# A transformer block with quantised feed-forward and routed experts: gathered token tiles transposed by DMA instead of TensorE

## The reference

```python
def reference(x, w1, w2, router_w, gate_proj, up_proj, down_proj):
    x = x + quantised_ffn(layernorm(x), w1, w2)     # per batch: int8 products of 512x512x512 and 512x256x512
    h = layernorm(x)
    p = softmax(h @ router_w)                       # 8 experts
    weights, chosen = top_k(p, 2)                   # 2 per token, weights normalised to 1
    for e in chosen experts of a token:
        x += weight[e] * ((silu(h @ gate_proj[e]) * (h @ up_proj[e])) @ down_proj[e])
    return x
```

## Time and profile before

| | us |
|---|---|
| median of 3 runs | 382.35 (381.81 to 384.08) |
| profiled execution | 381.06 |
| its span, first to last instruction | 379.3 |
| PE busy in the span | 321.9 |
| first late gather starts | 217.69 |
| last 12 matmuls of "up" (tile 38) start | 362.56 |

### The profile page before, as it was taken

How to read it: one execution, slowest core, us unless ns; L and a number is a source line. 1 busy time by engine, 2 the same in 40 slices (tenths; PEclk the granted TensorE clock), 3 DMA queues, 4 the chain that set the end, 5 groups by cost and what they waited for, 6 DMA issues and landing times.

```text
span 379.3 us, 6450 instructions
## 1 busy us (share of the span) xinstructions
PE 321.9 (85%) x1955; PEld 189.8 (50%) x1955; DVE 225.1 (59%) x515; ACT 202.9 (54%) x382; POOL 244.5 (64%) x271
## 2 busy tenths in 40 slices
PE   4698757877798885679899899999999999999980
PEld 1455435545665652375574455555555555555530
DVE  3588887879899988878678732333333333333320
ACT  1557568888897796139635234444444444444430
POOL 6486697879999971685461472656667746675441
PEclk9999999999999999999999999999999999999997
DMA  7765446745765508147127554557687657786544
GB/s 247 245 264 196 136 163 199 265 147 165 277 258 188 189 35 242 64 167 232 75 31 275 86 144 80 101 99 116 129 137 115 125 95 123 132 137 107 92 55 55
DMA packets 27551, 56.79 MB, mean 150 GB/s; under 512 B 2624, under 2 KB 13888, under 8 KB 25600
## 3 DMA queue, kind: packets, MB, share of 16 engines
q0 software_dynamic: 8736, 20.45, 29.9%
q1 hardware_dynamic: 17968, 35.39, 27.0%
q10 hardware_dynamic: 816, 0.54, 0.5%
HBM read 37.50 MB, written 18.87 MB: 149 GB/s over the span
## 4 chain that ended last, share of the span: by engine, by line
PE 33%; POOL 22%; issue 17%; DVE 14%; ACT 5%; DMA 4%; POOLq 2%; SPq 0%; DVEq 0%; ACTq 0%
PE bank_h L1328 13%; PE bank_q L1349 6%; POOL x L648 4%; POOL w_in L666 3%; POOL out L687 3%; DVE amax L726 3%; PE bank_t L1313 3%; PE bank_q L1194 2%; POOL w_in L619 2%; POOL gu_lo L584 2%; DVE rmax L756 2%; POOLq L682 2%; PE bank_h L1222 2%; ACT xn L1014 2%; DMA stage<-tokens,gather_at 2%
## 5 line engine op out<-in xcount | busy, mean ns | idle before, releaser
L1328 PE MATMUL bank_h<-gu_hi,xT 128*128 x312 | 103.9, 379 | 0.0
L1328 PE MATMUL bank_h<-gu_lo,xT 128*128 x156 | 59.1, 379 | 0.0
L970 DVE SCALAR_TENSOR_TENSOR xT<-bank_t,xT 128x512 f16<-128x512 f32 x39 | 26.8, 689 | 53.9 <-ACT xT L1104 53.8
L1349 PE MATMUL bank_q<-dn_hi,aT 128*128 x156 | 52.6, 379 | 1.7 <-DVE aT L988 1.4
L1328 PEld LDWEIGHTS bank_h<-gu_hi,xT 128*128 128x128 f16 x312 | 30.5, 98 | 29.3 <-issue 0.2
L666 POOL DMA_INDIRECT w_in<-tokens,gather_at x30 | 29.8, 993 | 17.8 <-issue 7.6
L584 POOL TENSOR_TENSOR gu_lo<-stage,gu_hi 128x1024 bf16<-128x1024 f32 x16 | 34.0, 2135 | 7.5 <-ACT gu_hi L1061 7.3
L978 DVE SCALAR_TENSOR_TENSOR gated<-bank_h,gated 128x256 f32<-128x256 f32 x39 | 16.5, 422 | 32.0 <-ACT gated L1111 32.0
L1111 ACT ACTIVATE gated<-bank_h 128x256 f32<-128x256 f32 x39 | 14.9, 383 | 38.0 <-PE bank_h L1328 38.0
L726 DVE TENSOR_REDUCE amax<-bank_t 128x1 f32<-128x512 f32 x48 | 30.8, 684 | 6.6 <-PE bank_t L1194 4.7
L687 POOL DMA_INDIRECT out<-h,scatter_at x17 | 26.9, 1580 | 11.8 <-DMA out<-h,scatter_at 4.5
(11 more groups left out here) (197 smaller groups left out, 704.5 us busy)
## 6 DMA issues: line engine op xcount, KB each, us to landing
stage<-in_L_ffn_gate_proj SPq DMA_DIRECT2D x8, 512.0 KB, 4.2
stage<-in_L_ffn_up_proj SPq DMA_DIRECT2D x8, 512.0 KB, 4.1
stage<-in_L_ffn_down_proj SPq DMA_DIRECT2D x8, 512.0 KB, 4.9
x<-in_x SPq DMA_DIRECT2D x4, 1024.0 KB, 6.3
out<-x SPq DMA_DIRECT2D x4, 1024.0 KB, 4.6
tokens<-xn SPq DMA_DIRECT2D x4, 1024.0 KB, 4.5
x_in<-in_x SPq DMA_DIRECT2D x3, 1024.0 KB, 7.5
w_in<-in_fside_BxS2xS SPq DMA_DIRECT2D x3, 1024.0 KB, 5.6
```

Of the source, the lines that this page charges most:

```text
L970: dve.scalar_tensor_tensor(out=xT[i % 2][:, 1].rearrange("p c t -> p (c t)"), in0=bank, scalar=X_SCALE, in1=xT[i % 2][:, 0].rearrange("p c ...
L1328: ins = pe.matmul(bank, xT[i % 2][:, part, c], rhs[:, cols], start=(c == 0 and m == 0), stop=(c == C - 1 and m == 2))
L1349: ins = pe.matmul(bank, aT[i % 2][:, part, c], rhs[:, cols], start=(c == 0 and n == 0), stop=(c == FC - 1 and n == 2))
```

## The change

`tokens_dram` has rows of 1024 float16: 512 of the high half, 512 of the low half; a row still has 2 KB. The scale 256 moves into the layer norm (`deviation` for part 2). After `normalise 2` of a batch, ACT makes the high halves of the whole batch (`token_high`, one instruction, 128x2048), and DVE (batches 0, 2, 3) or POOL (batch 1) makes the low halves in place (`token_low`, one instruction, 128x2048). SP stores the halves with two DMAs; all that waited for the store of a batch waits for both. ACT's `x_high`, DVE's `x_low` and PE's transposes of tokens are gone, 39 of each; PE's list keeps the step "expert", which only reads the expert's number.

In their place SP has the steps "turn": one DMA transpose each of a gathered tile, 128x1024 float16 to `xT` as eight blocks of 128x128. The ring `xT` has four buffers; two of them lie in the old `xqT`. Turn i waits for gather i and, from i = 4 on, for "up" of tile i-4. Gather i+4 of the late tiles waits for turn i, and an early gather i+3 for turn i. The landings are no longer counted at the end of SP's list but as steps "landed" between the turns.

```diff
-            def x_low(i):
-                ...
-                dve.scalar_tensor_tensor(out=xT[i % 2][:, 1].rearrange("p c t -> p (c t)"), in0=bank, scalar=X_SCALE,
-                                         in1=xT[i % 2][:, 0].rearrange("p c t -> p (c t)"), op0=ALU.mult,
-                                         op1=ALU.subtract).then_inc(ring_t.taken, 1)
+            def token_low(b):
+                dve.wait_ge(sem("token_high"), b + 1)
+                dve.tensor_tensor(token_low_of, xn2[:], token_high_of(b), ALU.subtract).then_inc(sem(f"token_low{b}"), 1)
...
+            def token_high(b):
+                if b == 1:
+                    ring_q.done(act, "x transposed", C - 1, B - 1)
+                elif b > 1:
+                    act.wait_ge(sem(f"tokens_stored{b - 1}"), 32)
+                act.wait_ge(sem("xn2_ready"), upto(b, J))
+                act.activation(token_high_of(b), xn2[:], ACT.Copy).then_inc(sem("token_high"), 1)
...
+            def turn(i):
+                sp.wait_ge(gathered(i), 16 * times_gathered(i))
+                if i == 0:
+                    sp.wait_ge(sem("xn_ready"), upto(B - 1, J))
+                if i == len(xT_in):
+                    ring_h.done(sp, "product 1", J - 1, B - 1)
+                if i >= TURNS:
+                    ring_h.done(sp, "up first", 0, i - TURNS)
+                sp.dma_start_transpose(xT[i % TURNS], xg(i)).then_inc(sem(f"turned{i % TURNS}"), 16)
...
+        held = []
+        for name, i in pool_order:
+            if name == "gather" and i >= EARLY:
+                sp_order += held
+                held = [("turn", i)]
+            elif name == "scatter" and i >= EARLY - 1:
+                if held and held[0][1] - TURNS < i:
+                    sp_order += held
+                    held = []
+                sp_order.append(("landed", i))
+        sp_order += held
```

The loop gives SP the late list: turns 9 to 17, landed 8, turn 18, landed 9, landed 10, turn 19, and so on; near the end it reads turn 33, landed 29, landed 30, turn 34, landed 31, turn 35, landed 32, turn 36, landed 33, turn 37, landed 34, turn 38. In the early lists, a line or two of the tables:

```diff
-    "store x1 1, load expert 22, load expert 23, load w2 3, load x again 2, store tokens 1, store x1 2, "
-    "store tokens 2, load x again 3, store tokens 3, store x1 3")
+    "expert 23, load w2 3, load x again 2, store tokens 1, store x1 2, turn 0, turn 1, turn 2, store tokens 2, load x "
+    "again 3, turn 3, turn 4, store x1 3, turn 5, turn 6, turn 7, store tokens 3, turn 8")
```

More of the change, by code:

```diff
@@ L335, in block_kernel @@
             x_in = inputs.enter_context(nc.sbuf_tensor("x_in", [P, J, D], F32))
-        xT = [tmp(f"xT{n}", [P, 2, C, P], F16) for n in range(2)]
+        xT_in = [tmp(f"xT{n}", [P, 2 * C, P], F16) for n in range(2)]
         gated = [tmp(f"gated{n}", [P, F], F32) for n in range(2)]
@@ L373, in block_kernel @@
         to_scatter = waiting + [("scatter", i) for i in range(EARLY, TILES)]
-        act_order.append(("x high", FIRST))
-        dve_order.append(("x low", FIRST))
         for i in range(EARLY, TILES):
@@ L384, in block_kernel @@
             if i + 1 < TILES:
-                pe_order.append(("x low", i + 1))
-                act_order.append(("x high", i + 1))
-                dve_order.append(("x low", i + 1))
+                pe_order.append(("expert", i + 1))
             pe_order += [("up first", i), ("a low", i - 1), ("up rest", i), ("take y", i - 1)]
@@ L409, in xg @@
         def xg(i):
-            return rows_of_stage[:, i % 3] if i < EARLY else w1_in[:, (i - EARLY) % J, 0:D]
+            return rows_of_stage[:, i % 3].bitcast(F16) if i < EARLY else halves[(i - EARLY) % J]
         def xg_before(i):
@@ L512, in _ @@
                 sp.wait_ge(sem(f"x1_stored{b}"), 16)
-            if EARLY:
-                sp.wait_ge(sem("added"), 16 * EARLY)
-            sp.sem_inc(sem("landed"), 1)
-            for i in range(EARLY, TILES):
-                n = i - EARLY
-                sp.wait_ge(sem(f"added{n % (2 * J)}"), 16 * (n // (2 * J) + 1))
-                sp.sem_inc(sem("landed"), 1)
         @block.gpsimd
@@ L593, in deviation @@
                     pool.wait_ge(sem("gap_ready"), group_of[b - 2] + 1)
-                pool.tensor_scalar(r, v[:, :, 1], LN_EPS, None, ALU.add).then_inc(done, 1)
+                if which == 0:
+                    pool.tensor_scalar(r, v[:, :, 1], LN_EPS, None, ALU.add).then_inc(done, 1)
+                else:
+                    pool.tensor_scalar(r, v[:, :, 1], LN_EPS, 1.0 / (X_SCALE * X_SCALE), ALU.add, ALU.mult).then_inc(done, 1)
                 pool.tensor_scalar(s, v[:, :, 0], -1.0, None, ALU.mult).then_inc(done, 1)
@@ L663, in gather @@
                 if before is not None:
-                    ring_t.done(pool, "x low", 0, before)
+                    pool.wait_ge(sem(f"turned{before % TURNS}"), 16 * (before // TURNS + 1))
                 rows = tokens_dram[0:T * len(GROUPS[0])] if i < EARLY else tokens_dram
@@ L1303, in _, with expert @@
             experts = {}
-            def transpose_x(i):
+            def expert(i):
                 if i == PHASES[phase_of[i]][1]:
@@ L1309, in transpose_x @@
                 experts[i] = pe.value_load(expert_at[0:1, i:i + 1], min_val=0, max_val=E - 1)
-                bank = ring_t.fill(pe, "x low", 0, i)
-                pe.wait_ge(gathered(i), 16 * times_gathered(i))
-                for c in range(C):
-                    ins = pe.transpose(bank[:, c * P:(c + 1) * P], xg(i)[:, c * P:(c + 1) * P], identf[:])
-                ins.then_inc(ring_t.filled, 1)
             def gate_up(half, i):
@@ L1327, in gate_up @@
                     for m, (part, rhs) in enumerate(((0, gu_hi_at), (0, gu_lo_at), (1, gu_hi_at))):
-                        ins = pe.matmul(bank, xT[i % 2][:, part, c], rhs[:, cols], start=(c == 0 and m == 0),
+                        ins = pe.matmul(bank, xT[i % TURNS][:, part * C + c], rhs[:, cols], start=(c == 0 and m == 0),
                                         stop=(c == C - 1 and m == 2))
@@ L1367, in _ @@
                      "tokens": tokens, "scores": router,
-                     "place": rank, "sort": partial(sort, 0), "table": partial(sort, 1), "indices": compact, "x low": transpose_x,
+                     "place": rank, "sort": partial(sort, 0), "table": partial(sort, 1), "indices": compact, "expert": expert,
                      "up first": partial(gate_up, 0), "up rest": partial(gate_up, 1), "a low": transpose_a, "take y": down})
```

76 lines of the change are left out of this document (46 added, 30 removed), and 89 rows, old and new, of tables (ACT_ORDER, DVE_ORDER, PE_ORDER, POOL_ORDER).

## The result

The changed kernel takes 416.68 us (median of 4 runs, 410.49 to 419.21) where the kernel before took 383.22 beside it (381.81 to 384.18). By the medians that is 33 us slower, above the top of the forecast range (412). The ratio is 1.078, with a 95% interval of 1.072 to 1.083, which is 30 us.

A forecast was written before the change was run, and what follows sets the result against it. PE was taken to bound the late tiles before, the scatter chain after; span 379.3 + 4.9 (chain, including the early loss) + 2.6 (landings) = 386.8, with 1.76 and 1.3 for execution and median 390 us, range 376 to 412.

The forecast's parts named there:

- 2.4 + 2 + 2 - 2: Up to gather 9: halves of batches 0, 2 and 3, less transposes and copies saved; about 4 us later, gather 9 at 221.7.
- 4.3 without that cover: POOL's low half of batch 1, ahead of the first gather: counted as nothing in an idle stretch, otherwise 4.3 us.
- A turn lands 4.1 us after its issue: Transposing DMA of a tile: latency taken from SP's 512 KB transfers, as no row showed a transposing DMA.
- the bounds: For a turn's landing after its issue: 2.7 us as the lower and 9.8 as the upper.
- The chain scatter, landing, turn: Late tiles: turns stand between landings in SP's list, so PE needs scatters four or five tiles ahead; span 4.9 us longer.
- scatter 30 keeps its distance: From scatter 9 to scatter 30 the old spacing stays, so scatter 30 starts 3.8 us later, at 339.7.
- the 0.2 us that I added to a landing: Slower landings beside 39 turns: 0.2 us on each of 13 in succession, 2.6 in all (bounds 0 and 0.5 each).
- PE as the bound: First rival, late tiles: turns land early and PE's whole saving arrives, 17.2 off and 4 for halves: 369 us; chance 0.11.
- the third: Third rival, late tiles: SP or DMA engines need over 4.1 us a turn without overlap, far slower; chance 0.14.
- its two prices: Third rival, late tiles: 397 us at 5 us a turn, 426 us at 6 us a turn.
- 261 GB/s: Rate of a DMA transpose in one kernel, by which a 256 KB turn would take an estimated 1.0 us.
- 1309 ns a block: For a 128x128 block: a turn's eight blocks would take an estimated 10.5 us if not overlapping; supports the third rival.

The follow-up runs named there:

- the average of four: Four kernels with the same early part (the changed one, direct waits, more matmuls while waiting, gathers ahead): gather 9 at 230.5 us on average, over a spread of 4.
- without halves: The changed kernel with no high or low halves computed and each batch stored in one transfer (tokens wrong): 404.90 us, gather 9 at 218.18.
- idle turns: The kernel before plus 30 transposing DMAs of 256 KB in the late tiles that nobody waits for: 394.22 us, 2.1% slower, late part 172.8.
- the mended order: The changed kernel with landings waited for directly, gathers 19 to 38 ahead of scatters, and fillers for the sort: 399.55 us, ratio 1.041, late part 171.3.
- copies: The changed kernel with plain DMAs of the same 256 KB in place of turns (expert part wrong): 396.37 us, ratio 1.036, late part 164.5.

## Why the prediction was wrong in size and right in direction

1. *PE bounds the kernel before and would need 4.10 a tile.* Right; where PE is not held up, tiles follow each other so ("up" of tile 33 starts at 365.94, of tile 32 at 361.83).
2. *The early part costs 4: 2.4 + 2 + 2 - 2, POOL's half nothing.* Measured 14.6 in the profiled execution, 12.8 on the average of four. The step that failed here is "POOL's low half of batch 1 lies in an idle stretch, I count nothing": the stretch is idle on POOL, not on DVE, and it cost 4.9 (the 3.74 for which `packed` was shut out, and what follows). My price "4.3 without that cover" was near it, but I gave it no chance. DVE's 2.4 for a batch was read from a row whose second input is a PSUM bank (`bank_r`, L774); the halves read both from SBUF, and took 2.28 without and 3.11 and 3.24 with POOL beside them. Batch 0 cost 1.8, and batches 2 and 3 the 4.0 I had, both no larger than the spread of 4. The 2 us for the transposes and copies that go did not come: without halves gather 9 was still 0.5 later than before.
3. *A turn lands 4.1 us after its issue.* 4.7 in the median, up to 8.4. It is inside the bounds, but I took for a latency what is also the DMA engines' time.
4. *The chain scatter, landing, turn.* The mechanism is there, link by link. The stages, forecast and measured: gather 9 to scatter 3, 9.9 and 11.4; to scatter 9, 31.0 and 33.4; to scatter 30, 77.1 and 86.0; to "up 34", 9.2 and 11.5; to "up 38", 18.6 and 25.8; to the end, 16.7 and 16.6. That is 22.2 more, of which 2.6 were in the sum for landings. The step that failed most is "scatter 30 keeps its distance" (8.9): it was read from a kernel in which the DMA engines had 0.31 of their time left. With it failed the 0.2 us that I added to a landing. Landings took 5.3 in the median, but the six of this stretch for which POOL waits, at a change of expert, took 6.4 on average against 5.3 before: 6.7 us of the 8.9. The longest, of scatter 21, took 7.8 with two turns beside it; POOL waited 6.4 there. POOL went on 0.1 us after each of them came, as before, so in this stretch SP's list delayed no count. The other (7.2) is the loop of tiles 34 to 38: 2.8 for turn 37 (6.87 against 4.1), 1.7 for "up 34" to scatter 33 (7.02 against 5.33), 2.9 for tile 37 (7.02 against 4.10), which PE made at the lower clock level after its wait, less 0.2 for the landing between.
5. *The rivals.* PE as the bound fell at once. Of the third, that turns need more than 4.1 us of a tile, a part holds: not SP and not a turn by itself (1.38), but turn and rest of a tile together need 4.5 to 4.9 us of the DMA engines. I put the condition on the turn alone, and gave the case 0.14. By "up 9" at 242.32 and "up 38" at 400.37 a tile took 5.45 us, between its two prices. Of the late loss of 23 us the DMA engines' load alone makes 11 (idle turns); the mended order takes 13 away and copies 20. The two causes overlap, so these parts are no sum.
6. *The Trainium skill's 261 GB/s ("DMA: Bandwidth & Descriptors", section "Latency and other measured facts") and its 1309 ns a block ("VectorE: DVE Perf Modes", section "The three transpose paths").* The trace agrees with neither as I used them: 190 GB/s with nothing beside it, and eight blocks every 1.38 us.

## What to carry to other kernels

Before work is moved to the DMA engines, add up their time per period of the pipeline as for any engine, including what they do already (0.69 of 4.54 us here), and price a transposing DMA like this one at twice a copy (1.38 against 0.66 us). An idle stretch on POOL was no cover while DVE worked on two SBUF operands (1.15 us became 4.89): look at both engines' rows at that time. Where a wait is put into an in-order list, follow the loop back to the waiting engine (turn, "up", `take y`, scatter, landing, turn) and divide its length by the tiles it carries; the distance of two events in an uncontended trace is not kept once the resource between them is full.

## What was unexpected of the hardware

- A transposing DMA of 128x1024 float16 within SBUF: 1.38 us at a share of 1.00, against 0.66 us for the copy; SP is held 1.23 us at least for the one and 0.46 for the other, and still 1.19 for a transposing DMA of half the size.
- DVE's 128x768 float16 pair of 1.15 us took 4.89 us beside one POOL instruction of 4.48 us. DVE's low half of batch 3, with POOL idle for its first 1.7 us, took 2.28 us; those of batches 0 and 2 took 3.11 and 3.24, and each started about 1 us before an instruction of POOL ended. It goes the other way too: beside the low half of batch 0, POOL's next instruction (109.11) took 4.05 us, where those of the same shape on either side of it took 2.13 and 2.14.
- Each of PE's two waits of over 4 us at the end was followed by "up" matmuls of 0.61 to 0.63 us instead of 0.38 (at tile 37 at once, at tile 34 from 0.9 us on): the granted clock's lower level. Yet holding the clock up with extra matmuls did not change the time.
